# Routing in a decoder layer: one pass after attention, or tile by tile inside it

## The reference

```python
x = x + self_attention(layernorm(x))             # 16 heads of 8, causal
x = x + cross_attention(layernorm(x), ctx)       # then relu(out @ W1 + b1) @ W2 + b2
x = x + ffn(layernorm(x)):
    h = x + rotary_attention(rmsnorm(x, g1))     # causal
    z = rmsnorm(h, g2)
    topw, topi = top_k(softmax(z @ w_router), 2) # 8 experts, weights divided by their sum
    y = h + sum over both choices of topw * ((silu(z @ wg[e]) * (z @ wu[e])) @ wd[e])   # 384 hidden
```

## Time and profile before

| | |
|---|---|
| median of three runs | 756.88 us |
| the profiled execution's own time | 758.17 us |
| its span, first to last instruction | 756.4 us |
| TensorE, weight loads, VectorE, ScalarE, GpSimd busy | 81%, 61%, 66%, 52%, 35% of the span |
| mean granted TensorE clock | 0.929 |
| last copy of logits | 507.63 us |
| first transposes of an expert block | 553.60 us |
| reload of results begins | 734.27 us |

### The profile page before, as it was taken

The page is one execution under the profiler, slowest core; times in us unless marked ns, Lnnn a source line. Parts: engine busy times, 40 slices in busy tenths (PEclk is TensorE's granted clock), DMA queues, the critical chain, the costliest instruction groups (busy, mean ns, idle before and its releaser), DMA issues. The chain is left out here.

```text
span 756.4 us, 28418 instructions
## 1 busy us (share of the span) xinstructions
PE 611.4 (81%) x11893; PEld 460.5 (61%) x11893; DVE 499.0 (66%) x1131; ACT 394.0 (52%) x831; POOL 267.3 (35%) x391
## 2 busy tenths in 40 slices
PE   4788999999989989898898889841469998988840
PEld 2355666666656565656655555630369987988840
DVE  3377688778777777777777687838826654555437
ACT  3255466555455555454645444451537765655525
POOL 4010110101121321322314241222567777777750
PEclk9599999999999999999999999975569999999985
DMA  4304400001000010010100001010031111111129
GB/s 129 109 18 159 125 18 17 28 22 34 6 27 27 7 55 16 28 45 28 44 17 13 34 17 45 31 56 1 26 129 53 50 54 54 51 52 55 51 76 303
DMA packets 35246, 39.88 MB, mean 53 GB/s; under 512 B 10256, under 2 KB 25424, under 8 KB 34992
## 3 DMA queue, kind: packets, MB, share of 16 engines
q1 hardware_dynamic: 30576, 28.74, 11.8%
q0 software_dynamic: 4544, 9.32, 4.3%
HBM read 20.80 MB, written 10.94 MB: 42 GB/s over the span
## 5 line engine op out<-in xcount | busy, mean ns | idle before, releaser
L1209 DVE TENSOR_REDUCE rmax<-ps_s 128x16 f32<-128x1024 f32 x96 | 117.2, 1221 | 82.2 <-PE ps_s L1019 81.6
L1082 ACT ACTIVATE probsT<-ring 128x512 f32<-128x512 f32 x192 | 103.8, 591 | 100.6 <-PE ring L1031 100.6
L1213 DVE TENSOR_TENSOR shifted<-ps_s,rmax 128x1024 f32<-128x1024 f32 x96 | 117.6, 1225 | 10.2 <-PE ring L1047 0.5
L665 PE MATMUL ps_s<-room 128*128 128x128 f32 x852 | 110.3, 281 | 0.0
L1031 PE MATMUL ring<-const,shifted 128*128 128x128 f32 x768 | 106.5, 282 | 1.1 <-DVE att L1225 1.1
L665 PEld LDWEIGHTS ps_s<-room 128*128 128x128 f32 x852 | 104.0, 197 | 0.0
L743 DVE SCALAR_TENSOR_TENSOR room<-room,ps_s 128x384 f32<-128x384 f32 x71 | 39.3, 554 | 80.2 <-ACT room L715 80.2
L1047 PEld LDWEIGHTS ring<-vbd,probsT 128*32 128x32 f32 x6144 | 62.3, 110 | 44.1 <-issue 39.6
L1031 PEld LDWEIGHTS ring<-const,shifted 128*128 128x128 f32 x768 | 83.8, 142 | 5.4 <-issue 1.1
L1335 POOL TENSOR_TENSOR pt<-mv,small 128x4 f32<-128x4 f32 x24 | 4.8, 200 | 217.8 <-DVE mv L1238 217.8
L610 POOL DMA_INDIRECT room<-hn_dram,gather_rows x71 | 68.8, 969 | 28.9 <-issue 20.1
(11 more groups left out here) (172 smaller groups left out, 916.4 us busy)
## 6 DMA issues: line engine op xcount, KB each, us to landing
room<-kS SPq DMA_DIRECT2D x96, 64.0 KB, 1.9
room<-y_dram SPq DMA_DIRECT2D x16, 256.0 KB, 5.7
room<-in_x SPq DMA_DIRECT2D x8, 256.0 KB, 3.3
hn_dram<-hn SPq DMA_DIRECT2D x8, 256.0 KB, 2.3
base_dram<-base SPq DMA_DIRECT2D x8, 256.0 KB, 2.4
room<-base_dram SPq DMA_DIRECT2D x1, 2048.0 KB, 7.8
out<-room SPq DMA_DIRECT2D x8, 256.0 KB, 4.9
cin<-in_ctx SPq DMA_DIRECT2D x8, 192.0 KB, 2.9
```

The source lines that it names most:

```text
L665: last = mm(bank[r][:, k * P:(k + 1) * P], w, xbT[r], start=True, stop=True)
L1082: nc.scalar.activation(probsT[p % 2][:, 4 * g:4 * g + 4, :], ring[u.bank][:].rearrange("p (k c) -> p k c", c=P), ACT.Exp, scale=SCALE)\
L1209: V.reduce_max(rmax[p % 2][:].rearrange("p (g k) -> p g k", g=GROUPS), ps_s, AX.X).then_inc(rmax_ready, 1)
L1213: V.tensor_tensor(shifted[p % 2][:].rearrange("p (g k) s -> p g k s", g=GROUPS), ps_s, rmax[p % 2][:].rearrange("p (g k) -> p g k", g=GROU ...
```

## The change

Each expert gets a fixed region of 33 blocks in a DRAM tensor `moved_dram`, with rows of 130 numbers: 128 features, the row of `y_dram` where the result goes (an integer), and half the choice's weight. For every rotary tile:

- step `lg`: VectorE (`choose_dve`) makes both choices for 4 subtiles, their sum `sel` and running counts `carried`;
- a new step `rk` on TensorE, which takes a PSUM bank in turn: two products give each choice's row; ScalarE takes an exponential; VectorE (`place_dve`) writes positions, target rows and weights into `moved`;
- at `ap2` GpSimd also copies the scaled rows, so that both choices have a full row; `base` is gone and the sum goes into `xs[t]` in place;
- new steps `s0` to `s3` on GpSimd: two indirect scatters each, 128 rows, into the regions.

`rk` stands at pair 1 of the job two behind, `s0` and `s1` at pairs 2 and 3, `s2` and `s3` at pair 1 of the job three behind. Inversion, exports and `residual`'s reload are gone. After the walk `tables_dve` works out the expert and base row of the 71 blocks, SyncE stores padding rows behind each expert's last row (addresses read from `pad_at`), then loads each block with a plain DMA whose address it reads from `base_at`. The buffer `xb` holds the target rows until the block's results are stored, so it is loaded again behind `y_stored`. Results are multiplied with the row's weight as they are copied. At the end VectorE only adds.

```diff
-2: ROTARY: (((), ("lg",)), ((), ()), ((), ()), ((), ()))
+2: ROTARY: (((), ("lg",)), ((), ("rk",)), ((), ("s0",)), ((), ("s1",)))
+-3: ROTARY: (((), ()), ((), ("s2", "s3")), ((), ()), ((), ()))
...
+    last = N_JOBS - 1
+    yield "lg", last - 1
+    yield "s2", last - 2
+    yield "s3", last - 2
+    yield "oT", last
+    yield "wo", last
+    yield "rk", last - 1
+    yield "st2", last
+    yield "ap2", last
+    for name in MOVES:
+        yield name, last - 1
+    for name in ("hT", "lg", "rk") + MOVES:
+        yield name, last
...
+        for k, src in enumerate((logits, second)):
+            in_turn(dve, V.reduce_max(top[:, k, :], src[:], AX.X))
+            in_turn(dve, V.tensor_tensor(less[:], src[:], wide(top[:, k, :]), ALU.is_lt))
+            in_turn(dve, V.scalar_tensor_tensor(keyed[:], less[:], float(EXPERTS), iota, ALU.mult, ALU.add))
+            in_turn(dve, V.tensor_reduce(first_at[:, k, :], keyed[:], AX.X, ALU.min))
+            in_turn(dve, V.tensor_tensor(chosen[:, k], iota, wide(first_at[:, k, :]), ALU.is_equal))
+            if k == 0:
+                in_turn(dve, V.scalar_tensor_tensor(second[:], chosen[:, 0], -1e30, logits[:], ALU.mult, ALU.add))
+        V.tensor_tensor(gap[:], top[:, 1, :], top[:, 0, :], ALU.subtract).then_inc(gap_ready, 1)
+        V.tensor_copy(carried[:, 0, :], region_at[:] if t == 0 else carried[:, SUB, :])
+        in_turn(dve, V.tensor_tensor(sel[:], chosen[:, 0], chosen[:, 1], ALU.add))
+        for s in range(SUB):
+            add = V.tensor_tensor(carried[:, s + 1, :], carried[:, s, :], sel[:, s, :], ALU.add)
...
+            elif name == "rk":
+                mm(rank, const[:, C_LOW:C_LOW + P], sel[:], start=True, stop=False)
+                last = mm(rank, ones[:], carried[:, 0:SUB, :], start=False, stop=True)
...
+        V.tensor_tensor(at_expert[:], chosen[:], rank..., ALU.mult)
+        in_turn(dve, V.reduce_sum(pos_f[:], at_expert[:], AX.X))
+        V.tensor_copy(pos_i[r][:], pos_f[:])
+        V.tensor_copy(moved[r][:].bitcast(I32)[:, :, :, E], rows)
+        dve.wait_ge(weight_ready, t + 1)
+        in_turn(dve, V.tensor_scalar(wsum[:], w1st[:], 2.0, 2.0, ALU.mult, ALU.add))
+        in_turn(dve, V.reciprocal(moved[r][:, 0, :, E + 1], wsum[:]))
+        V.tensor_tensor(moved[r][:, 1, :, E + 1], w1st[:], moved[r][:, 0, :, E + 1], ALU.mult)
...
+                G.tensor_tensor(xs[t], hres[:], xs[t], ALU.add).then_inc(base_ready, 1)
+                pool.wait_ge(normed, NORMS["st2", n])
+                wait(pool, rows_moved[t % 2], MOVED * (t // 2))
+                G.tensor_copy(moved[t % 2][:, 1, :, 0:E], hn[t % 2]).then_inc(doubled, 1)
+            elif name in MOVES:
+                pool.wait_ge(rows_known, t + 1)
+                pool.wait_ge(doubled, t + 1)
+                for k in range(2):
+                    G.indirect_dma_start(out=moved_dram, in_=moved[t % 2][:, k, s, :], ...)
...
+        for e in range(EXPERTS):
+            at = sp.value_load(pad_at[0:1, e:e + 1], ...)
+            sp.dma_start(moved_dram[bass.ds(at, P), :], pads[:, e, :]).then_inc(pads_stored, 16)
+        for j in range(USED):
+            if j >= UNROLL:
+                sp.wait_ge(y_stored[r], 16 * (j // UNROLL))
+            at = sp.value_load(base_at[0:1, j:j + 1], ...)
+            sp.dma_start(xb[r], moved_dram[bass.ds(at, P), :]).then_inc(xb_loaded[r], 16)
...
+        for j in range(USED):
+            pool.wait_ge(y_copied, j + 1)
+            G.indirect_dma_start(out=y_dram, in_=yb[r], ..., ap=xb[r].bitcast(I32)[:, E:E + 1])
...
-            V.tensor_scalar(yb[r], y_bank[c % 2], 0.5, None, ALU.mult).then_inc(y_copied, 1)
+            V.tensor_scalar(yb[r], y_bank[c % 2], xb[r][:, E + 1:E + 2], None, ALU.mult).then_inc(y_copied, 1)
...
+            V.tensor_tensor(y0[:, sl, :], y0[:, sl, :], residual[:, sl, :], ALU.add)
+            V.tensor_tensor(residual[:, sl, :], y0[:, sl, :], y1[:, sl, :], ALU.add)
```

More of the change, by code:

```diff
@@ L281, in _build @@
     xh = sb("xh", [P, SUB, E])
-    hn = sb("hn", [P, SUB, E])
+    moved = [sb(f"moved{r}", [P, 2, SUB, ROW]) for r in range(2)]
+    hn = [moved[r][:, 0, :, 0:E] for r in range(2)]
     hres = sb("hres", [P, SUB, E])
-    base = sb("base", [P, SUB, E])
     stats = sb("stats", [P, SUB, 6])
@@ new lines, in tables_dve, with wide @@
+        block = const[0:1, C_BLK:C_BLK + BLOCKS]
+        def wide(x):
+            return x.unsqueeze(1).broadcast_to([1, BLOCKS, EXPERTS])
+        in_turn(dve, V.tensor_tensor(past[:, 0], block.unsqueeze(2).broadcast_to([1, BLOCKS, EXPERTS]), wide(ends),
+                                     ALU.is_ge))
+        V.reduce_sum(past_sum[:, 0], past[:, 0], AX.X)
+        in_turn(dve, V.tensor_tensor(past[:, 1], past[:, 0], wide(blocks_f[:, 2, :]), ALU.mult))
+        in_turn(dve, V.reduce_sum(past_sum[:, 1], past[:, 1], AX.X))
@@ L654, in rows_T @@
             later(pe, xbT_copied, i * UNROLL + c)
-            nc.tensor.transpose(x_bank, xb[r], ident).then_inc(xbT_filled, 1)
+            nc.tensor.transpose(x_bank, xb[r][:, 0:E], ident).then_inc(xbT_filled, 1)
         def gate_up(i, c):
@@ L969, in use @@
             elif name == "hT":
-                last = transposes(ps_g, hn)
+                last = transposes(ps_g, hn[t % 2])
             elif name == "wo":
@@ L985, in use @@
                     last = mm(ps_g[:, s * EXPERTS:(s + 1) * EXPERTS], hT[:, s * P:(s + 1) * P], w_r[:],
+                              start=True, stop=True)
+            elif name == "rk":
+                rank = ps_g[:, 0:SUB * EXPERTS].rearrange("p (s e) -> p s e", s=SUB)
+                mm(rank, const[:, C_LOW:C_LOW + P], sel[:], start=True, stop=False)
+                last = mm(rank, ones[:], carried[:, 0:SUB, :], start=False, stop=True)
+                if t == TILES - 1:
+                    last = mm(ps_g[:, SUB * EXPERTS:(SUB + 1) * EXPERTS], ones[:], carried[:, SUB, :],
                               start=True, stop=True)
@@ L1109, in apply_rms @@
             act.wait_ge(factors_ready, m)
[L1110 removed]
+            wait(act, rows_moved[t % 2], MOVED * (t // 2))
             for s in range(SUB):
[L1112 removed]
+                last = nc.scalar.activation(hn[t % 2][:, s, :], hres[:, s, :], ACT.Copy, scale=rstd[m % 2][:, s:s + 1])
             last.then_inc(normed, 1)
```

392 lines of the change are left out of this document (146 added, 246 removed).

## The result

The changed kernel took 752.7 us (median of 5 runs, 751.71 to 754.07) beside 756.78 us for the kernel before on the same chip (755.98 to 757.3). The ratio is 0.9948, interval 0.9933 to 0.9963. It is faster by about 0.5%, not by the 3.3% that was forecast, and 752.7 lies above the range of 722 to 751. The profiled execution took 752.70 us, with a span of 750.9.

A forecast was written before the change was run, and what follows sets the result against it. Bounds by stage: TensorE and VectorE alternating in attention, then routing and inversion, GpSimd's gathers and scatters in the experts, DMA at the end. 756.4 + 18.6 - 20.9 - 22.0 - 1.0 = 731.1 us span, forecast 732, range 722 to 751.

The forecast's parts named there:

- part 1: Attention: routing adds 4.8 us of VectorE work per tile, partly covered by idle time; 3.1 us per tile, +18.6 us.
- third rival: Attention: VectorE's lumps stop the loop longer through the four-buffer bank rotation, +36 instead of +18.6, 749 us; chance 0.22.
- part 2: Row moves on GpSimd during attention: 1.28 us each, 10.2 us per tile, six tiles' worth costed at nothing.
- rival of dear moves: End of attention: the 16 last moves cost 3.2 us each and GpSimd becomes the bound, 763 us; chance 0.08.
- part 3: Between attention and experts: 46.0 us of routing and inversion removed, first rows at TensorE 532.7 instead of 553.6, -20.9 us.
- part 4: Experts: GpSimd issues only scatters, so TensorE sets the pace at 2.12 us per step to the end, -22.0 us.
- ring of eight: Experts: SyncE's loads wait for a store eight blocks back, 2.38 us per block, +18, 750 us; chance 0.15.
- part 5: Return of results: DMA traffic of 6 MB sets this stage, only the last tile's wait shrinks, -1 us.

The follow-up runs named there:

- run with lumps alone: Kernel before the change plus useless small vector instructions in the places of the choice and the placing, nothing else: 785.77 us, ratio 1.0334.
- best version: Changed kernel with routing cut into pieces, its steps last in their place, moves started early and ranks one place later: 730.58 us, ratio 0.9636.
- experiments 6 and 7: Changed kernel with the choice cut up: 753.37 us; routing's steps also last in their place: 744.67 us; then ranks, weights and moves earlier too: 733.55 us.
- experiment 3: Changed kernel with four useless 128x512 products per tile added on TensorE ahead of the ranks, tiles 0 to 5: 747.03 us, ratio 0.9857.

## Why the prediction was wrong

**Attention (part 1 of the working), the step that failed.** It priced 4.8 us of vector work per tile nearly right: the choice takes 3.8 us and the placing 1.5. It then took 1.1 to 2.9 us of VectorE's idle time as cover for it. As the work stands in the changed kernel, that cover was not used. VectorE's idle time before the row maxima, summed over the same pairs of both kernels (44 and 43 of them; groups of instructions, before and after), has not become less:

```profile
L1209 DVE TENSOR_REDUCE rmax<-ps_s 128x16 f32<-128x1024 f32 x44 | 53.6, 1219 | 29.1 <-PE ps_s L1019 28.9
```

```profile
L1145 DVE TENSOR_REDUCE rmax<-ps_s 128x16 f32<-128x1024 f32 x43 | 52.3, 1216 | 29.7 <-PE ps_s L962 29.7
```

VectorE waits there for scores, and the scores wait for what VectorE does before; when it is later, they are later, and the wait comes again. The run with lumps alone gives 25.8 us for what this step put at 18.6, already above it, and it has no ranks in it. There the same idle time is 22.7 us, so some 6 us of it, 1 us a tile, did serve as cover.

The idle time is not lost for good, though. In the best version the same group, over the same pairs (265 to 500 us), reads

```profile
L1167 DVE TENSOR_REDUCE rmax<-ps_s 128x16 f32<-128x1024 f32 x43 | 52.4, 1219 | 18.3 <-PE ps_s L984 18.1
```

which is 11 us less than before, for the same instructions, and attention is 10 us late instead of 39. So idle time can cover vector work, but not a lump that stands ahead of the work for the next scores, and it was such a lump that the sum laid against it.

**Left out of the sum:** the ring's turn (7.0 us, or 7.7 since tile 0) and the clock. The working priced the rank products at half a microsecond, and not the order of the buffers, in which one more turn gives the projection the buffer that VectorE empties late. The third rival had this mechanism, "a bank that VectorE frees late holds the output projection", with +36 us and 749 us. It came at +38.5 and 752.7: this rival is in the main what happened, and its chance of 0.22 was too low. That its number is so close is in part luck: it put the lumps at their full length, which is more than they cost, and left out the clock. That the clock would fall behind the stops was in no case.

**Moves on GpSimd (part 2)** were priced right: the 64 moves take 0.98 us on average and 0.30 before each, 1.28 as forecast. "Six tiles' worth I cost at nothing" was wrong by the 3.4 us of tile 2, inside the 5 us named for it. The rival of dear moves fell: none took longer than 1.20 us. The copy of the normed rows took 0.61 us, not 1.27.

**The seam (part 3)** held: -21.5 for -20.9, with the same last in line. The 16 moves of the last two tiles go out one behind the other (the first at 546.51, the last at 565.54), and TensorE sees rows 5.1 us after the last begins, where 2.3 + 0.4 + 2.3 = 5.0 had been put. The parts of these 5.1 us are others: the first load is issued 3.1 us after the last move begins, where 2.7 had been put, and its rows are there 1.95 us later, not 2.3. The end of the moves moved with their start in experiments 6 and 7. But the moves are not alone there, as the working had it: SyncE's stores of padding go out 1.16 us apart (0.9 in the working), the last at 565.6, beside the last move at 565.54, and the loads wait for both. The moves land 2.4 us after their issue and these stores 1.8 (medians), so by an estimate faster moves alone would have ended the seam only 0.5 us earlier; no run separates the two.

**The experts (part 4)** held: -20.5 for -22.0. Steps are 2.12 us apart, TensorE is busy for 91.84 of 92 us between 620 and 712, GpSimd for 41.24, or 45%. TensorE waits for a block's rows once behind the second block, for 0.15 us (before 683.74), so the ring of eight did not bind; this rival fell.

**The end (part 5)** gave 2.1 us instead of 1.0, within its ends.

So the sum was 756.4 + 38.5 - 21.5 - 20.5 - 2.1 = 750.8 (750.9 measured), and the 19.8 us by which the span was missed are the 19.9 us of the first term.

## What to carry to other kernels

Where two engines alternate, price a lump of instructions added to either at close to its full length (three quarters and more here), whatever idle time the rows show beside it. Where buffers go round in turn, write down which step gets whose buffer once a use is added: the one that pays can be another step than the new one. Cut such work into pieces, put each behind whatever the next turn needs, and start early what feeds a queue that will be the bound later: the same instructions in other places gave 3% here. A stop of TensorE should be priced with the half clock behind it, read from the windows.

## What the runs showed of the hardware

Behind a stop of TensorE of 3.25 us the granted clock was 0.50 for about 5 us of the work that followed, and 3.6 us of useless products, which with the ranks filled the time of that stop, removed this. In the kernel with lumps alone, a stop of 2.73 us before 280.87 left it at 1.00, while at stops of 2.31 and 2.36 us later it fell: the length of the stop alone does not decide.

A small vector instruction can be held by GpSimd. In the best version the conversion of the positions, 0.17 us at tiles 0 and 4, takes 0.96 us three times and ends within 0.03 us of a GpSimd addition of 1.27 us that reads and writes 128x512 (order of time on VectorE; the addition starts at 351.45, 393.30 and 440.36):

```profile
351.79 0.96 DVE L505 CAST pos_i<-pos_f 128x8 int32<-128x8 f32 x1
...
393.64 0.96 DVE L505 CAST pos_i<-pos_f 128x8 int32<-128x8 f32 x1
...
440.69 0.96 DVE L505 CAST pos_i<-pos_f 128x8 int32<-128x8 f32 x1
```

The Trainium skill, "SBUF — State Buffer", section "Who interferes with whom", says that VectorE and GpSimd share a pair of ports, that a VectorE cast can take both, and that the one that issues first keeps them for its whole instruction. These rows agree for VectorE as the one that is blocked; they cost 0.8 us each, and the one of experiment 3, beside an addition from 280.84 to 282.11, 1.1 us. The reverse, which the prediction allowed for with 3 us, did not show: the moves of the last tile kept to 0.96 us and 0.30 between, also while VectorE's small instructions for the tables ran.

Left open: the 1.3 us of attention that no run isolates; what the clock alone costs in the changed kernel, since the useless products remove it at some of the tiles only; which of the moves and the stores of padding ends the seam; and a buffer of its own for the ranks, which was not tried, since all eight are in use.
